# Experts, layer 1 and the last stages of a two-layer decoder in one program instead of two

## What is computed

```python
x = x + L0_self_attention(layernorm(x))            # first program, not touched
x = x + L0_cross_attention(layernorm(x), ctx)      # first program, not touched
# experts: a base product and eight low-rank experts under a gate
h = layernorm(x); gate = softmax(h @ W_gate.T); thr = sigmoid(h @ W_thr + b_thr) / 8
w = where(gate >= thr, gate - thr, 0); w = w / sum(w)
x = x + h @ W_base.T + b_base + 2 * einsum(h @ A.T, w, B)
# layer 1: causal-free self attention, 32 query heads, 8 key heads, head size 16
x = x + softmax(q @ k.T / 4) @ v @ Wo.T            # q, k, v from layernorm(x)
# last stages: cross attention on ctx, then a product with a matrix of signs
x = x + softmax((h @ Wq.T + bq) @ (ctx @ Wk.T + bk).T / sqrt(512)) @ ctx
x = x + (layernorm(x) @ sign) * softplus(scale)
```

## Time and profile before

| | us |
|---|---|
| median of 3 runs (lowest, highest) | 1042.51 (1042.32, 1046.19) |
| the profiled execution's own time | 1042.14 |
| its span, first to last instruction | 1040.4 |
| mean granted clock of PE | 0.954 of full |
| busy: PE, DVE, ACT, POOL | 913.6 (88%), 843.9 (81%), 637.4 (61%), 682.8 (66%) |
| first product of the second program | 736.78 |
| first product of the third program | 831.73 |
| batch 7 of layer 1 added to `x` | 980.41 |

### The profile page before, as it was taken

How to read it: one execution, slowest core, us unless ns; L and a number is a source line. 1 busy time by engine, 2 the same in 40 slices (tenths; PEclk the granted TensorE clock), 3 DMA queues, 4 the chain that set the end, 5 groups by cost and what they waited for, 6 DMA issues and landing times. The chain is left out here.

```text
span 1040.4 us, 21446 instructions
## 1 busy us (share of the span) xinstructions
PE 913.6 (88%) x6396; PEld 469.8 (45%) x6504; DVE 843.9 (81%) x2090; ACT 637.4 (61%) x1784; POOL 682.8 (66%) x686
## 2 busy tenths in 40 slices
PE   4789997799989999999999999997669989898477
PEld 2345543444444555555555555543335445555143
DVE  7998997699966898999999998994785547677495
ACT  4678887734455666766666666763432259888350
POOL 5798988777764666666666666661781456565483
PEclk9789998899999999999999999999889979998789
DMA  8699999964643667555555556554521459777556
GB/s 338 132 204 158 166 166 189 200 112 82 131 92 102 123 122 122 123 121 121 121 122 121 121 121 123 122 122 101 142 42 21 122 96 154 137 140 139 134 96 142
DMA packets 384304, 136.32 MB, mean 131 GB/s; under 512 B 369760, under 2 KB 370400, under 8 KB 381792
## 3 DMA queue, kind: packets, MB, share of 16 engines
q1 hardware_dynamic: 384224, 135.39, 63.6%
HBM read 42.01 MB, written 2.10 MB: 42 GB/s over the span
## 5 line engine op out<-in xcount | busy, mean ns | idle before, releaser
L156 PE MATMUL bank<-w_hi,hT 128*128 128x512 f16 (+2 forms) x1024 | 324.2, 372 | 18.1 <-DVE w_lo L388 3.7
L156 PE MATMUL bank<-w_hi,small 128*128 128x512 f16 x512 | 162.8, 379 | 9.1 <-DVE small L1540 8.0
L156 PE MATMUL bank<-w_lo,hT 128*128 128x512 bf16 (+2 forms) x465 | 170.5, 369 | 0.0
L820 ACT ACTIVATE big<-bank,small 128x128 f32<-128x128 f32 x512 | 145.6, 386 | 29.7 <-DVE small L922 28.9
L156 PEld LDWEIGHTS bank<-w_hi,hT 128*128 128x128 f16 (+1 forms) x1024 | 100.6, 99 | 121.8 <-issue 17.8
L1366 POOL TENSOR_TENSOR small<-small,mhalf 128x4 f32<-128x4 f32 x64 | 64.5, 1008 | 130.4 <-DVE small L963 130.3
L676 POOL TENSOR_TENSOR big<-big 128x512 f16<-128x512 f32 x96 | 115.8, 1212 | 37.3 <-DVE big L931 19.8
L156 PE MATMUL bank<-small,big 128*128 128x17 f16 (+2 forms) x1728 | 106.4, 194 | 13.3 <-DMA big<-big 7.9
L922 DVE TENSOR_REDUCE small<-bank 128x4 f32<-128x512 f32 x128 | 86.7, 685 | 37.2 <-PE bank L728 36.1
L1467 ACT ACTIVATE small<-small 128x128 f32<-128x128 f32 x256 | 98.8, 390 | 0.0
L156 PEld LDWEIGHTS bank<-small,big 128*128 128x128 f16 (+1 forms) x1728 | 69.0, 97 | 59.5 <-DMA big<-big 12.7
(11 more groups left out here) (198 smaller groups left out, 2040.2 us busy)
## 6 DMA issues: line engine op xcount, KB each, us to landing
stage<-in_weights SPq DMA_DIRECT2D x16, 1024.0 KB, 6.4
stage<-in_weights SPq DMA_DIRECT2D x64, 256.0 KB, 2.9
big<-big SPq DMA_TRANSPOSE x168, 3.4
small<-in_ctxT SPq DMA_DIRECT2D x2, 1024.0 KB, 8.4
big<-in_ctx SPq DMA_DIRECT2D x2, 1024.0 KB, 7.1
out<-x SPq DMA_DIRECT2D x8, 256.0 KB, 2.7
big<-in_vectors SPq DMA_DIRECT2D x5, 256.0 KB, 11.4
x<-in_x SPq DMA_DIRECT2D x2, 512.0 KB, 4.7
```

Of the source, the lines that this page charges most:

```text
L156: last = nc.tensor.matmul(out, lhs(a, c), rhs(b, c), start=start and n == 0, stop=stop and n == 3 * chunks - 1)
L820: last = nc.scalar.activation(group(prob, n)[:, i * P:(i + 1) * P], S[n % len(S)][:, i * P:(i + 1) * P], ACT.Exp, bias=nmax[:, m:m + 1])
```

## The change

The second and the third program become one (`second_half`), so one barrier less. `experts` becomes a class `Experts` with one method an engine; it serves as layer 1's `opening`. `SECOND_ORDER` is one list for each engine that holds the experts' steps and the whole fill of layer 1 mixed (rounds -3 to 0); the loop's rounds 1 to 4 and their body stay as they are. `END_ORDER` is one list for each engine that holds layer 1's drain, the eight `g` with their evictions, and all of the last stages mixed; `ending` walks it. The `bias` products stand behind the eight `key` products, ahead of layer 1; the `g` products stand in the drain.

The cut diff (lists shortened to the parts spoken of):

```diff
-EXPERTS_ORDER = {
-    "tensor": """
-        key_0 key_1 key_2 base_0 base_1 gates_0 key_3 gates_1 key_4 share_turn_0 key_5 key_6 key_7 share_turn_1 up_0
-        up_1 g_0 g_1 g_2 g_3 g_4 g_5 gates_2 gates_3 base_2 up_2 share_turn_2 base_3 base_4 up_3 up_4 share_turn_3
-        base_5 up_5 base_6 up_6 base_7 up_7 g_6 g_7 bias_0 bias_1
+SECOND_ORDER = {
+    "tensor": """
+        key_0_0 key_1_0 key_2_0 gates_0_0 base_0_0 key_3_0 key_4_0 share_turn_0_0 gates_1_0 up_0_0 base_1_0 key_5_0
+        up_1_0 key_6_0 key_7_0 gates_2_0 base_2_0 bias_0_0 bias_1_0 share_turn_1_0 base_3_0 q_0_0 q_1_0 up_2_0 q_2_0
+        q_3_0 up_3_0 share_turn_2_0 k_0_0 k_1_0 k_2_0 k_3_0 gates_3_0 q_0_1 base_4_0 up_4_0 q_1_1 q_2_1 q_3_1 scores_0_0
+        scores_1_0 base_5_0 scores_2_0 share_turn_3_0 base_6_0 scores_3_0 p_turn_1_0 scores_4_0 up_5_0 k_0_1 k_1_1
+        up_6_0 k_2_1 k_3_1 scores_5_0 base_7_0 scores_6_0 pv_0_0 pv_1_0 up_7_0 scores_7_0 q_0_2 p_turn_4_0 q_1_2 q_2_2
...
+        pv_5_1 p_turn_1_2 k_2_3 pv_6_1 pv_7_1 out_1_0 scores_4_2 out_2_0 k_3_3 out_3_0 scores_5_2 pv_0_2
...
+    "gpsimd": """
+        in_root_0_0 lxk_lo_pool_1_0 in_lo_0_0 in_root_1_0 in_root_2_0 in_lo_1_0 in_root_3_0 x_bias_0_0 in_lo_2_0
+        in_root_4_0 w_lo_0_0 x_bias_1_0 in_lo_3_0 in_root_5_0 in_lo_4_0 w_lo_1_0 x_bias_2_0 lxq_lo_0_0 lxq_lo_1_0
...
+    "sync": """
+        small_load_0_0 load_0_0 in_turn_0_0 in_turn_1_0 in_turn_2_0 in_turn_3_0 in_turn_4_0 load_1_0 load_2_0
+        in_turn_5_0 out_turn_0_0 out_turn_1_0 in_turn_6_0 in_turn_7_0 k_turn_0_0 q_turn_0_0 out_turn_2_0 q_turn_1_0
+        q_turn_0_1 p_turn_0_0 out_turn_3_0 p_turn_2_0 load_3_0 k_turn_0_1 p_turn_3_0 p_turn_5_0 q_turn_1_1 p_turn_6_0
...
+class Experts:
...
+        self.GB, self.Y, self.T = (chip.psum[1], chip.psum[7]), (chip.psum[6], chip.psum[5]), chip.psum[4]
+        self.KB, self.G = (chip.psum[0], chip.psum[2], chip.psum[3]), (chip.psum[0], chip.psum[5])
...
+        self.background = Splitting(chip, sem, 0, self.staged, 4, name="coming")
```

In `self_attention` (layer 1 now takes an opening, and batch 0 waits where banks and buffers are shared with the experts; batch 7 has one bank for its turned probabilities):

```diff
+            if what == "ow_lo":
+                at = slice(n * D, (n + 1) * D)
+                pool.wait_ge(o_weight_hi, n + 1)
...
+                if begins(b) and n == 0:
+                    pe.wait_ge(opening.background.done, 2 if what == "q" else 4)
+                    pe.wait_ge(opening.wide_lo, NB + 2)
...
+                    if begins(b) and n == 0:
+                        pe.wait_ge(opening.up_added, NB - 1)
+                    if begins(b) and n == 4:
+                        pe.wait_ge(opening.gates_taken, NB // 2)
...
-        return T[by_pe.index(g) % 2]
+    def bank_of(g, b):
+        return T[0 if ends(b) else by_pe.index(g) % 2]
...
+                if begins(b):
+                    dve.wait_ge(opening.y_done, NB)
```

```diff
-LAST_ORDER = {
-    "tensor": """
-        scores_0 scores_1 prob_turn_0 pv_0 scores_2 prob_turn_1 scores_3 pv_1 prob_turn_2 prob_turn_3 scores_4 pv_2
-        scores_5 pv_3 prob_turn_4 prob_turn_5 scores_6 pv_4 pv_5 scores_7 sign_0 prob_turn_6 prob_turn_7 sign_1 pv_6
-        pv_7 sign_2 sign_3 sign_4 sign_5 sign_6 sign_7
+END_ORDER = {
+    "tensor": """
+        pv_1_6 scores_6_6 p_turn_4_6 scores_7_6 g_0_0 pv_2_6 pv_3_6 scores_0_7 scores_1_7 pv_4_6 g_1_0 p_turn_7_6
+        scores_2_7 g_2_0 out_0_5 scores_3_7 pv_5_6 p_turn_1_7 pv_6_6 g_3_0 scores_4_7 out_1_5 scores_5_7 out_2_5 pv_7_6
+        pv_0_7 pv_1_7 scores_6_7 g_4_0 scores_7_7 p_turn_4_7 out_3_5 g_5_0 g_6_0 pv_2_7 pv_3_7 g_7_0 p_turn_7_7 pv_4_7
+        pv_5_7 pv_6_7 pv_7_7 out_0_6 out_1_6 out_2_6 last_scores_0_0 out_3_6 last_scores_1_0 last_prob_turn_0_0
+        last_scores_2_0 last_pv_0_0 out_0_7 out_1_7 out_2_7 out_3_7 last_scores_3_0 last_prob_turn_1_0
+        last_prob_turn_2_0 last_scores_4_0 last_pv_1_0 last_prob_turn_3_0 last_pv_2_0 last_prob_turn_4_0 last_scores_5_0
+        last_scores_6_0 last_pv_3_0 last_sign_0_0 last_prob_turn_5_0 last_pv_4_0 last_prob_turn_6_0 last_pv_5_0
+        last_scores_7_0 last_sign_1_0 last_prob_turn_7_0 last_pv_6_0 last_sign_2_0 last_pv_7_0 last_sign_3_0
+        last_sign_4_0 last_sign_5_0 last_sign_6_0 last_sign_7_0
...
-        experts(chip, 2, 3, 4, 5, 0, [W_L1O, W_SIGN])
-        run(chip, lambda sem: second_layer(chip, sem))
+        run(chip, lambda sem: second_half(chip, sem))
```

More of the change, by code:

```diff
@@ L548, in self_attention @@
     batch0 = lambda b: first and isinstance(b, int) and b == 0
-    staged = list(chip.n_staged) if opening is None else [s + 16 for s in opening.staged]
+    begins = lambda b: not first and isinstance(b, int) and b == 0
+    ends = lambda b: not first and isinstance(b, int) and b == NB - 1
+    staged = [s + 16 for s in opening.staged]
     background = Splitting(chip, sem, coming, staged, NB, None if first else 1)
@@ L554, in schedule @@
     def schedule(eng, name, step):
[L556 to L571, removed]
+        own = {"sync": opening.sync, "gpsimd": opening.gpsimd, "tensor": opening.tensor, "scalar": opening.scalar,
+               "vector": opening.vector}[name]
+        for what, n, b in opening.order[name]:
+            own(eng, what, n, b)
+            step(what, n, b)
+        if name == "tensor":
+            opening.wait_rows(eng, NB - 1)
         with eng.Fori(1, NB - far) as it:
@@ L754, in step @@
                     opening.wait_rows(pe, 1)
-                turn(chip, bank_of(n), group(prob, n)).then_inc(p_in_bank, 1)
+                if begins(b) and by_pe.index(n) < 2:
+                    if by_pe.index(n) == 0:
+                        pe.wait_ge(opening.s_lo, NB // 2)
+                    else:
+                        pe.wait_ge(opening.up_added, NB)
+                turn(chip, bank_of(n, b), group(prob, n)).then_inc(p_in_bank, 1)
             if what == "out":
@@ L776, in scalar @@
     def scalar(act):
-        if not first:
-            act.wait_ge(chip.staged[0], staged[0])
-            nc.scalar.activation(chip.weight(slots["o"])[0], chip.stage[:, 0, :], ACT.Copy).then_inc(o_weight_hi, 1)
-            act.wait_ge(prepared, setups)
         def step(what, n, b):
+            if what == "ow_hi":
+                if n == 0:
+                    act.wait_ge(chip.staged[0], staged[0])
+                    act.wait_ge(opening.wide_done, NB)
+                at = slice(n * D, (n + 1) * D)
+                nc.scalar.activation(chip.weight(slots["o"])[0][:, at], chip.stage[:, 0, at],
+                                     ACT.Copy).then_inc(o_weight_hi, 1)
             if what in ("q_hi", "k_hi"):
@@ L856, in prepare @@
                                       ).then_inc(prepared, 1)
-        if not first:
-            for n in range(2):
-                prepare(n)
-            for t in (qs, ks):
-                nc.vector.memset(t, 0.0).then_inc(prepared, 1)
-            dve.wait_ge(prepared, setups)
         def step(what, n, b):
@@ L949, in self_attention @@
                    s_done=s_done, v_done=v_done, out_done=out_done, background=background.done)
-    if opening is not None:
+    if first:
         signals["ctx_lo"] = opening.ctx_lo
@@ L2032, with last_stages @@
     """,
 }
-def last_stages(chip, sem, sign_slot, seen):
+def last_stages(chip, sem, sign_slot, seen, rows):
     nc, io = chip.nc, chip.io
-    order = {name: stages(text) for name, text in LAST_ORDER.items()}
-    g, r, ident = late_views(chip)
+    g, r, ident = rows.g, rows.r, rows.ident
     WIDE = NB * P
@@ L2061, in last_stages @@
                          "attended", "inv", "x_added", "signed", "added"))
-    def schedule(name, step):
-        for what, b, _ in order[name]:
-            step(what, b)
     def two(x, b, width=P):
```

810 lines of the change are left out of this document (445 added, 365 removed).

## The result

Four runs of the changed kernel took 1008.13 to 1008.84 us, median **1008.63**. Beside them the kernel before took a median of 1044.35 (the three runs of its table and a fourth of 1052.55); the ratio is **0.9643, 95% interval 0.9589 to 0.9697**. The forecast was 1006. The profiled execution took 1008.13 us with a span of 1006.4, against 1042.14 and 1040.4 before, so 34.0 us of span are to be explained.

A forecast was written before the change was run, and what follows sets the result against it. Three limits: experts near PE's limit, layer 1's fill and drain with nothing else in the lists, last stages waiting for turned rows. 1042.5 - 35.0 (ahead of the loop) - 1.4 (behind it) = 1006 us; range 988 to 1024.

The forecast's parts named there:

- Front: First `key` to layer 1's loop: at 12% idle, `x_add_0` at 849.1 for 884.1, 35.0 us less; bounds 43.3 and 23.8.
- the sum of PE's work, 98.8: From first `key` to layer 1's loop: products sum to 96.8 us, plus about 2 for first products at the low clock.
- Two of my signs of being wrong: Ahead of layer 1's loop: share chains of 8 us before `up`; right would be DVE and POOL busy sums no larger.
- g's leaving: Ahead of layer 1's loop: the eight `g` products leave, 20.8 us of PE's work.
- Loop: Layer 1's four rounds, body not edited: 62.5 us, 15.6 each, no change.
- Drain: Layer 1 behind its loop, with `g`: 45.0 us of PE work takes 48.4 in place of 30.8, 17.6 more.
- Tail: Behind `out_3_7`, the last stages: 37.5 us in place of 56.5, 19.0 less; bounds 33 and 42.
- The step named: Last stages: the DVE bunch goes, since first rows 0 to 6 are normalised before layer 1 has ended.
- Rival of POOL and DVE excluding each other: Ahead of layer 1's loop: two more share chains stretched by 6.4 us each, 12.8 together, total 1019; chance 0.18.
- Rival of better closed gaps: Ahead of layer 1's loop 7% idle, clock staying at 2.4 GHz, and the drain's low end: total 994; chance 0.19.
- Rival that it doesn't do what it says: Layer 1's fill: `pv_0_0` waits so long for `up_6` that the fill is as late as before: 1042; chance 0.04.
- the slower one: Layer 1's fill: PE queue stops at `q_0_0` until row 0 comes turned at about 811 us: 1055; chance 0.04.

The follow-up runs named there:

- the two runs with the front undone: Changed kernel with experts and layer 1's fill again one behind the other: 0.9839 of before; the same with the end's list also in old order: 1.0049.
- The two undone halves: Changed kernel with one list in old order: experts and layer 1's fill, 0.9839 of before; or layer 1's drain, g and last stages, 0.9837.
- the two halves of the end: Changed kernel with only g mixed into layer 1's drain, 0.9775 of before; with only the last stages' early steps mixed in, 0.9895.

## Why the prediction was right, step by step

The time was 2.6 us off, but its terms were further off than that: the front won 4.7 less than forecast, the loop lost 1.5, the drain grew 5.9 less, the tail won 1.8 less. That the two largest errors cancel is luck; that the change pays, and in the front and the tail, is what the working said.

- **Front: -35.0 predicted, -30.3 measured** (`x_add_0` 884.1 to 853.9), inside the bounds of -43.3 and -23.8. The share of PE's time, 88%, was right (0.90). What failed is the sum of PE's work, 98.8: it was 104.3. I said the clock would be 1.00 nearly throughout and put 2 us for its low stretch; it was 0.90. The front has three stretches at half clock in which PE works, 737.8 to 743.5, 763.7 to 767.6 and 832.3 to 842.5, with 19.3 us busy. At most half of that is the clock's doing, 9.6, so up to 7.6 more than I had put: by this estimate the clock is enough for the whole 5.5. The first `key` at 737.8 stayed, and the first `q` of batch 0 follows the base product that starts at 789.84, some 2.6 later, so 792 against my 785 to 790. Two of my signs of being wrong came: share chains of 8 us on the way to `up` (PE waits 7.3 us for the first two, of 11.7 idle in the front), and DVE busier than before, 99.5 us for 97.3 where I had 93.7; the scalings of rows alone take 999 ns each for 856.
- **What the front's gain is made of was only partly seen.** In my working g's leaving was 20.8 of PE's work, the larger part of 35. By the two runs with the front undone it is 8 to 9 with the barrier, up to 15 without my list's 6; mixing two streams that each had long waits of their own gives 13 to 22.
- **Loop: 0 predicted, +1.5 measured**, of it +3.0 in the first round (19.1 for 16.1) and -1.3 in the second (15.1 for 16.3); the last two are as before. With the old order in front the loop takes 62.0 and 62.6 us, with the mixed one never under 63.6, so the longer loop goes with the mixed front; why isn't shown.
- **Drain: +17.6 predicted, +11.7 measured.** The list's length was right and the 30.8 that it replaces was not. The list that I summed begins with `pv_1` of batch 6. On PE that step starts at 944.51 before and at 915.83 after, not at the 949.6 from which I counted the old drain. Start of that step and the drain from it on, before and after:

```profile
944.51 0.45 PE L156 MATMUL bank<-small,big 128*128 128x17 f16 x12
915.83 0.45 PE L157 MATMUL bank<-z,big 128*128 128x17 f16 x12
...
944.51:980.41 35.90, 24.47 (x273) 14.00 (x275) 16.71 (x34) 21.19 (x66) 15.92 (x21) 0.81 0.68 132
915.83:963.38 47.55, 44.67 (x423) 24.98 (x422) 36.00 (x82) 33.29 (x90) 29.92 (x37) 0.96 0.81 150
```

  PE's work is 44.7 us for my 45.0, the length 47.6 for my 48.4, the share busy 0.94 as taken. Against 35.9 that is 11.7 more; 5.1 of the 5.9 us of error are the wrong border. What my working didn't have is why the layer's own products, 23.0 us at clock 0.80 in the old drain, cost about what my full-clock prices say: g lifts it. And the drain isn't PE's alone: without three quarters of g it is as long.
- **Tail: -19.0 predicted, -17.2 measured** (39.2 for my 37.5, to the last `out`). The step named, that DVE's bunch and the 12.4 us wait go, held: 2.3 left. That g must be in the drain for this to pay I had not seen: with g behind it the tail is 73.0.
- **Rival of POOL and DVE excluding each other** (1019). Its first half is true. The share chains took 8.35 and 8.15 beside POOL, 2.2 and 4.9 later. What my rows left out is that the second chain was stretched before too, to 6.1. By the rule of the Trainium skill (SBUF — State Buffer, "Who interferes with whom"), that a VectorE instruction with two SBUF inputs and a GpSimd one that reads SBUF contend, moving GpSimd's copies should shorten the first chain; the trace agrees, with 5.1 us for 8.35. The rival's price was wrong: chains of 23.6 in place of 19.1 together are 4.5 more, not 12.8, and bringing the first turn 3.1 forward moved no end.

The timeline of DVE in the changed kernel has the same step of the chain beside POOL's copies, in the first chain, and alone, in the third:

```profile
755.91 1.84 DVE L2016 TENSOR_TENSOR small<-small 128x16 f32<-128x16 f32 x1
...
792.52 0.18 DVE L2016 TENSOR_TENSOR small<-small 128x16 f32<-128x16 f32 x1
```

It is ten times as long in the first. That is dear for the chain and cheap for the kernel.

- **Rival of better closed gaps** (994). It didn't come. The front's idle share was 10%, nearer my 12% than its 7%, and its condition, a clock that stays up, failed (0.90). Its sum was also off: the drain's low end takes away 4.8, not 8.
- **Rival that it doesn't do what it says, and the slower one.** Neither came. `q_0_0` had 19 us of slack to the 811 from which it would have decided.

## What to carry to other kernels

Work moved into a gap is not free and not full price: run both moves and each alone. Here g in the drain was worth 4.5 us, the last stages' early steps there -9.4, and both 17.9, because, as I read it, the one fills PE and the other removes the wait that would come next. A stretch whose engine is 94% busy can still be set by a chain of equal length: take work away to see it, and look at the clock while doing so. Price a list from the step with which it begins on its engine: my border 5 us behind that was one of the two largest errors here. And a join of programs with moved work is worth nothing by itself (1.0049): look for the gain in the order.

## What the runs showed that I had not expected

- **More work, higher clock, less time for each product.** The same 24 `out` matmuls of the drain took 518 ns each at clock 0.81 with a quarter of g beside them, 424 at 0.96 with all of it, and 380 at 1.00 with all of g and none of the last stages' steps. But fifteen matmuls of no use in the front's gaps only put off the fall of the clock by 3.1 us, and no time was won.
- **The clock falls without a long wait.** At 832.3 us it went to half after a stretch (820.0 to 832.2) in which PE was busy 9.5 of 12.2 us and none of its waits was over 0.94. With the gaps filled it fell at 837.0 after ten microseconds with 8.6 busy and no wait over 0.7.
- **The two undone halves add** (17.9 and 22.3, together 40.0 in one profile each; 1.004 and 1.0049 by the ratios), while the two halves of the end don't add at all.
